# A fused GNN layer on one core: TensorE's step reordered, with ScalarE's step reordered to match

## What is computed

```python
h = relu(layernorm(x))
for t in range(4):                            # edge type
    m = relu(concat(h[src], h[dst]) @ W1[t] + b1[t]) @ W2[t] + b2[t]
    msgs += where(edge_type == t, m, 0)
agg = segment_sum(msgs, dst, num_segments=100000)
i_r, i_z, i_n = split(agg @ W_ih.T + b_ih, 3)
h_r, h_z, h_n = split(h @ W_hh.T + b_hh, 3)
r, z = sigmoid(i_r + h_r), sigmoid(i_z + h_z)
n = tanh(i_n + r * h_n)
out = x + (1 - z) * n + z * h
```

## Time and profile before

| | before |
|---|---|
| median of 3 runs | 1842.27 us (1839.33 to 1843.18) |
| profiled execution: its own time | 1840.2 us |
| its span | 1838.3 us |
| granted TensorE clock, mean | 0.995 |
| PE / DVE / ACT / POOL busy | 91% / 87% / 81% / 64% of the span |
| PE's share of the chain that ended last | 73% |
| data moved | 319.72 MB, 174 GB/s on average |

### The profile page before, as it was taken

One profiled execution on the slowest core, in us unless ns is written; L12 is line 12 of the kernel. 1 busy time (PEld: TensorE's weight loads), 2 busy tenths in 40 slices (PEclk: granted clock), 3 DMA queues, 4 the chain that ended last, 5 costly groups with the idle time before them and its releaser, 6 DMA issues.

```text
span 1838.3 us, 43100 instructions
## 1 busy us (share of the span) xinstructions
PE 1667.1 (91%) x10182; PEld 1416.6 (77%) x10182; DVE 1595.2 (87%) x4186; ACT 1494.6 (81%) x3401; POOL 1178.9 (64%) x1982
## 2 busy tenths in 40 slices
PE   0226799999999999999999999999999999999998
PEld 0125688888888888888888888888888888888787
DVE  8597798989888988898889888989899989898776
ACT  0025789889888898898888888889898889888795
POOL 5777777776776777777765656666666566666310
PEclk9999899999999999999999999999999999999999
DMA  2225677777777776777677777777777777777653
GB/s 70 51 48 139 168 195 194 192 192 192 198 187 193 191 194 186 187 192 191 187 193 187 190 188 187 187 190 189 189 190 188 190 186 192 189 187 191 161 136 100
DMA packets 477071, 319.72 MB, mean 174 GB/s; under 512 B 106705, under 2 KB 463009, under 8 KB 476962
## 3 DMA queue, kind: packets, MB, share of 16 engines
q10 hardware_dynamic: 261792, 156.12, 28.6%
q1 hardware_dynamic: 185730, 106.99, 25.3%
q0 software_dynamic: 29440, 55.47, 11.8%
HBM read 211.65 MB, written 106.72 MB: 173 GB/s over the span
## 4 chain that ended last, share of the span: by engine, by line
PE 73%; ACT 8%; issue 4%; ACTq 3%; DVE 2%; DMA 0%; SPq 0%; POOL 0%; DVEq 0%; POOLq 0%
PE bank L1329 16%; PE bank L1331 12%; PE bank L1330 12%; PE bank L1409 10%; PE bank L1399 5%; PE bank L1391 5%; PE bank L1421 3%; PE bank L1420 3%; PE bank L1437 3%; ACT n_h L1194 3%; PE bank L1447 3%; ACT n_zc L1282 2%; ACTq L1211 2%; ACT e_r L1270 2%; ACTq L1232 2%
## 5 line engine op out<-in xcount | busy, mean ns | idle before, releaser
L580 POOL DMA_INDIRECT e_x<-in_x,rows_now x816 | 799.6, 980 | 241.7 <-issue 233.4
L1177 ACT ACTIVATE e_h<-e_x,shift,rstd 128x128 f32<-128x128 f32 x816 | 355.3, 493 | 93.6 <-DVE shift L1048 93.6
L1194 ACT ACTIVATE n_h<-n_x,shift,rstd 128x128 f32<-128x128 f32 x784 | 362.8, 489 | 2.1 <-issue 2.1
L1329 PE MATMUL bank<-n_h_hi,whh_hi 128*128 128x512 f32 x588 | 263.0, 447 | 25.3 <-ACT n_zc L1282 18.3
L1113 DVE TENSOR_TENSOR n_d<-bank,n_n 128x512 f32<-128x512 f32 x196 | 135.5, 691 | 160.7 <-ACT n_n L1278 149.1
L1329 PE MATMUL bank<-n_a_hi,wih_hi 128*128 128x512 f32 x588 | 249.3, 424 | 0.9 <-DVE bank L1083 0.9
L1071 DVE TENSOR_SCALAR n_sel<-iota,n_rel 128x256 fp32r<-128x256 f32 x784 | 237.8, 365 | 8.6 <-POOL n_rel L631 7.2
L1409 PE MATMUL bank<-n_sel,n_win 128*128 128x256 f32 x1568 | 234.9, 292 | 8.6 <-DVE n_sel L1071 8.4
L1331 PE MATMUL bank<-n_h_hi,whh_lo 128*128 128x512 f32 x588 | 232.9, 396 | 0.0
L1330 PE MATMUL bank<-n_h_lo,whh_hi 128*128 128x512 f32 x588 | 232.7, 396 | 0.0
L1331 PE MATMUL bank<-n_a_hi,wih_lo 128*128 128x512 f32 x588 | 232.3, 395 | 0.0
(11 more groups left out here) (179 smaller groups left out, 3895.4 us busy)
## 6 DMA issues: line engine op xcount, KB each, us to landing
n_win<-messages SPq DMA_DIRECT2D x1568, 64.2 KB
messages<-e_msg ACTq DMA_DIRECT2D x204, 257.0 KB, 2.7
n_x<-in_x ACTq DMA_DIRECT2D x195, 256.0 KB
out<-n_out ACTq DMA_DIRECT2D x195, 256.0 KB
e_x<-in_x,rows_now POOLq DMA_INDIRECT x816
rows_now<-lists SPq DMA_DIRECT2D x204, 2.0 KB
lists<-picks,list_rows POOLq DMA_INDIRECT x72
w<-in_W SPq DMA_DIRECT2D x1, 512.0 KB, 4.5
```

Source lines behind the costliest of these rows:

```text
L580: G.indirect_dma_start(e_x[:, s, 2 * end + t, :], None, x, bass.IndirectOffsetOnAxis(ap=rows_now[:, s, t, end:end + 1], axis=0)).then_inc( ...
L1177: last = A.activation(e_h[:, s % 2, k, :], e_x[:, s, k, :], ACT.Relu, scale=rstd[:, slot, col + k:col + k + 1], bias=shift[:, slot, col + ...
L1194: last = A.activation(n_h[:, s % 2, cols], n_x[:, s, cols], ACT.Relu, scale=rstd[:, slot, col + 4 + k:col + 5 + k], bias=shift[:, slot, co ...
L1329: T.matmul(o, w_hi, v_hi, start=start, stop=False, skip_group_check=onto)
```

## The change

TensorE's step becomes: r gate, hn; node transposes, window sums; z gate, n's second half; hid; back; edge transposes; message. The edge transposes move behind back, z moves ahead of n's second half, both move ahead of hid, and back moves ahead of the message.

ScalarE's step becomes: message copy e_msg (of the unit before: it moves from the end of a step to the start of the next); e_h tiles 0 to 2; n_r; e_h tile 3; store_messages; n_h_hi (it waits for n's second half of the group before instead of for z, as that now comes last of the two); n_h tile 0; n_a_hi; store_out, load_x; n_h tiles 1 and 2; n_zc; n_h tile 3; n_n (tanh); e_r; e_ht. No instruction is added or taken away, and each keeps its semaphores.

```diff
--- before.py
+++ after.py
@@ -1233,6 +1233,12 @@
                                   n_out[:, s, :].rearrange("p (k d) -> p k d", k=TILES)).then_inc(n_stored[s], 16)
 
             def step(i, m):
+                q, s = i - 10, (m - 10) % UNROLL
+                if within(q, UNITS):
+                    act.wait_ge(e_messaged, q + 1)
+                    act.wait_ge(e_tagged, q + 1)
+                    A.activation(e_msg[:, s, :, 0:D], bank[BE1][:, message_part].rearrange("p (t d) -> p t d", t=2),
+                                 ACT.Copy).then_inc(e_high, 1)
                 normalise_edges(i, m, (0, 1, 2))
                 g, s = i - LAG, (m - LAG) % 2
                 if within(g, NG):
@@ -1242,23 +1248,32 @@
                     A.activation(n_r[:, s, :], bank[BRZ][:], ACT.Sigmoid, bias=bsum[:, 0:1]).then_inc(n_red, 1)
                 normalise_edges(i, m, (3,))
                 store_messages(i, m)
-                q, s = i - 8, (m - 8) % 2
-                if within(q, UNITS):
-                    act.wait_ge(e_turned, q + 1)
-                    if due(q - 1):
-                        act.wait_ge(e_hid, q - 1)
-                    A.activation(e_ht[:, s, :], bank[BE0][:], ACT.Copy).then_inc(e_evaced, 1)
                 g, s = i - LAG + 1, (m - LAG + 1) % 2
                 if within(g, NG):
                     act.wait_ge(n_turned, g + 1)
                     if due(g - 1):
-                        act.wait_ge(n_gate_z, g - 1)
+                        act.wait_ge(n_gate_in, g - 1)
                     A.activation(n_h_hi[:, s, :], bank[BT[s]][:], ACT.Copy).then_inc(n_hhi, 1)
+                normalise_nodes(i, m, (0,))
+                if within(g, NG):
                     act.wait_ge(n_summed, g + 1)
                     A.activation(n_a_hi[:, s, :], bank[BA][:], ACT.Copy).then_inc(n_ahi, 1)
-                normalise_nodes(i, m, (0,))
                 store_out(i, m)
                 load_x(i, m)
+                normalise_nodes(i, m, (1, 2))
+                g, s = i - LAG, (m - LAG) % 2
+                if within(g, NG):
+                    act.wait_ge(n_gate_z, g + 1)
+                    if due(g - 1):
+                        act.wait_ge(n_eed, g - 1)
+                    A.activation(n_zc[:, s, :], bank[BRZ][:], ACT.Sigmoid, bias=bneg[:, 1:2],
+                                 scale=-1.0).then_inc(n_zed, 1)
+                normalise_nodes(i, m, (3,))
+                if within(g, NG):
+                    act.wait_ge(n_gate_in, g + 1)
+                    if due(g - 1):
+                        act.wait_ge(n_ded, g - 1)
+                    A.activation(n_n[:, s, :], bank[BIN][:], ACT.Tanh, bias=bih[:, 2:3]).then_inc(n_ned, 1)
                 q, s = i - 9, (m - 9) % 2
                 if within(q, UNITS):
                     act.wait_ge(e_hid, q + 1)
@@ -1269,25 +1284,12 @@
                         kind = 2 * ((m - 9) % 2) + t
                         last = A.activation(e_r[:, s, cols], bank[BE1][:, cols], ACT.Relu, bias=b1_cols[:, kind:kind + 1])
                     last.then_inc(e_relued, 1)
-                normalise_nodes(i, m, (1, 2))
-                g, s = i - LAG, (m - LAG) % 2
-                if within(g, NG):
-                    act.wait_ge(n_gate_in, g + 1)
-                    if due(g - 1):
-                        act.wait_ge(n_ded, g - 1)
-                    A.activation(n_n[:, s, :], bank[BIN][:], ACT.Tanh, bias=bih[:, 2:3]).then_inc(n_ned, 1)
-                    act.wait_ge(n_gate_z, g + 1)
-                    if due(g - 1):
-                        act.wait_ge(n_eed, g - 1)
-                    A.activation(n_zc[:, s, :], bank[BRZ][:], ACT.Sigmoid, bias=bneg[:, 1:2],
-                                 scale=-1.0).then_inc(n_zed, 1)
-                normalise_nodes(i, m, (3,))
-                q, s = i - 9, (m - 9) % UNROLL
+                q, s = i - 8, (m - 8) % 2
                 if within(q, UNITS):
-                    act.wait_ge(e_messaged, q + 1)
-                    act.wait_ge(e_tagged, q + 1)
-                    A.activation(e_msg[:, s, :, 0:D], bank[BE1][:, message_part].rearrange("p (t d) -> p t d", t=2),
-                                 ACT.Copy).then_inc(e_high, 1)
+                    act.wait_ge(e_turned, q + 1)
+                    if due(q - 1):
+                        act.wait_ge(e_hid, q - 1)
+                    A.activation(e_ht[:, s, :], bank[BE0][:], ACT.Copy).then_inc(e_evaced, 1)
 
             pipeline(nc, act, LAST, LOOP_END, step)
 
@@ -1382,14 +1384,6 @@
                     elif due(g):
                         pe.wait_ge(n_ted, g)
                     gate(BHN, 2, s, "h").then_inc(n_gate_hn, 1)
-                q, s = i - 8, (m - 8) % 2
-                if within(q, UNITS):
-                    pe.wait_ge(e_normed, q + 1)
-                    if due(q):
-                        pe.wait_ge(e_evaced, q)
-                    for k in range(4):
-                        last = T.transpose(bank[BE0][:, k * P:(k + 1) * P], e_h[:, s, k, :], ident[:])
-                    last.then_inc(e_turned, 1)
                 g, s = i - LAG + 1, (m - LAG + 1) % 2
                 if within(g, NG):
                     pe.wait_ge(n_normed, g + 1)
@@ -1409,6 +1403,12 @@
                             last = T.matmul(o, n_win[:, w, k, part_ * D:(part_ + 1) * D], n_sel[:, s, k, :],
                                             start=n == 0, stop=n == 3)
                     last.then_inc(n_summed, 1)
+                g, s = i - LAG, (m - LAG) % 2
+                if within(g, NG):
+                    pe.wait_ge(n_red, g + 1)
+                    gate(BRZ, 1, s, "ha").then_inc(n_gate_z, 1)
+                    pe.wait_ge(n_ted, g + 1)
+                    gate(BIN, 2, s, "a", onto=True).then_inc(n_gate_in, 1)
                 q, s = i - 9, (m - 9) % 2
                 if within(q, UNITS):
                     pe.wait_ge(e_evaced, q + 1)
@@ -1420,12 +1420,24 @@
                         T.matmul(o, w1[:, kind, 0, :], e_ht[:, s, t * P:(t + 1) * P], start=True, stop=False)
                         last = T.matmul(o, w1[:, kind, 1, :], e_ht[:, s, (2 + t) * P:(3 + t) * P], start=False, stop=True)
                     last.then_inc(e_hid, 1)
-                g, s = i - LAG, (m - LAG) % 2
-                if within(g, NG):
-                    pe.wait_ge(n_ted, g + 1)
-                    gate(BIN, 2, s, "a", onto=True).then_inc(n_gate_in, 1)
-                    pe.wait_ge(n_red, g + 1)
-                    gate(BRZ, 1, s, "ha").then_inc(n_gate_z, 1)
+                g, s = i - LAG - 1, (m - LAG - 1) % 2
+                if within(g, NG):
+                    pe.wait_ge(n_eed, g + 1)
+                    if within(g + 1, NG):
+                        pe.wait_ge(n_ted, g + 2)
+                    elif due(g):
+                        pe.wait_ge(n_outed, g)
+                    for k in range(TILES):
+                        last = T.transpose(bank[BHN][:, k * P:(k + 1) * P], n_e[:, s, k * P:(k + 1) * P], ident[:])
+                    last.then_inc(n_back, 1)
+                q, s = i - 8, (m - 8) % 2
+                if within(q, UNITS):
+                    pe.wait_ge(e_normed, q + 1)
+                    if due(q):
+                        pe.wait_ge(e_evaced, q)
+                    for k in range(4):
+                        last = T.transpose(bank[BE0][:, k * P:(k + 1) * P], e_h[:, s, k, :], ident[:])
+                    last.then_inc(e_turned, 1)
                 q, s = i - 9, (m - 9) % 2
                 if within(q, UNITS):
                     pe.wait_ge(e_relued, q + 1)
@@ -1436,16 +1448,6 @@
                         o = bank[BE1][:, 2 * P + t * D:2 * P + (t + 1) * D]
                         last = T.matmul(o, e_r[:, s, t * P:(t + 1) * P], w2[:, first + t, :], start=False, stop=t == 1)
                     last.then_inc(e_messaged, 1)
-                g, s = i - LAG - 1, (m - LAG - 1) % 2
-                if within(g, NG):
-                    pe.wait_ge(n_eed, g + 1)
-                    if within(g + 1, NG):
-                        pe.wait_ge(n_ted, g + 2)
-                    elif due(g):
-                        pe.wait_ge(n_outed, g)
-                    for k in range(TILES):
-                        last = T.transpose(bank[BHN][:, k * P:(k + 1) * P], n_e[:, s, k * P:(k + 1) * P], ident[:])
-                    last.then_inc(n_back, 1)
                 if isinstance(i, int) and i == CHECK_STEP:
                     pe.wait_ge(s_odd, 1)
                     T.matmul(bank[BT[0]][0:1, 0:1], ones128[:, 0:1], odd_sum[:], start=True, stop=True
```

## The result

The kernel after takes 1885.41 us (median of 4 runs, 1883.38 to 1887.53) beside 1842.19 us of the kernel before: a ratio of 1.0237, 95% interval 1.022 to 1.0255. It is slower by 43 us; the forecast was 70 us slower. The profiled spans say the same, 1881.5 us against 1838.3 us.

What follows compares the result with a forecast made beforehand. A closed ring of 8.35 us a step bounds the kernel; the new ring sums to 8.66, adding 49 us in the loop, 18 in the head and 3 after it: +70, forecast 1912 us, range 1868 to 1950.

Steps and rivals of the forecast that it cites:

- the sum: New ring in a loop step, from message products through sums, n_a_hi and e_r: 8.66 us against 8.35, averaging 8.72.
- Both rings: Old ring through n_zc (8.35 us) and new ring through the message (8.66), each holding the transfers' issue time.
- The time from n_a_hi to the next activation: On ScalarE, over both issues: 1.31 less 0.10 makes 1.21 us in the loop step, 1.06 in the head.
- The reaction of TensorE to e_r: From e_r's end on ScalarE to the message on TensorE: 0.15 us in the new ring.
- Part (a): z gate and n_zc early: cuts the ring through n_zc, worth at most 0.25 us a step if nothing replaces it.
- Part (e): TensorE's hn weight load: its 132 waits for n_out in the loop, 36.4 us, go away.
- Part (d): Message copy first on ScalarE, with VectorE's e_low: costed at nothing, ready at 4.36 against 4.39 by TensorE's way.
- Rival 1: Second ring through VectorE's n_sel, margin 0.12 us: another 20 to 35 us, 1932 to 1947; chance 0.14.
- Rival 2: Issues hidden, n_a_hi to n_h 0.49, ring 7.94 us, under TensorE's own 8.10: 1800 us; chance 0.08.
- Rival 3: n_h tile 1 comes 0.83 to 0.92 us after n_a_hi, ring 8.28 to 8.37: 1835 to 1880 us; chance 0.13.
- rival 4: Orders written for both engines do not bind, since each semaphore comes early anyway: 1842 us; chance 0.03.
- The signs named for a right forecast: Loop steps 8.65 to 8.75; TensorE waiting 0.3 to 0.5 for e_r; ScalarE idle 0.6 by issue; n_zc, n_out waits gone.

Runs made afterwards that it cites:

- run 2: Kernel after, with load_x alone moved from behind store_out to behind n_zc: 1814.38 us, ratio to before 0.9848.
- run 8: Kernel after, with TensorE's four edge transposes back ahead of the node transposes: 1954.72 us, ratio 1.0632.
- run 6: Kernel after, with n_h tile 0 back behind n_a_hi, ahead of the two issues: 1896.09 us, ratio 1.0299.
- run 3: Kernel after, with store_out and load_x moved from behind n_a_hi to the end of ScalarE's step, behind e_ht: 1865.69 us, ratio to before 1.0127.
- run 7: Kernel after, with ScalarE's e_r moved ahead of the tanh n_n: 1977.27 us, ratio 1.0732.
- run 1: Kernel before, with load_x alone moved from behind store_out to behind the tanh n_n: 1780.59 us, ratio to the kernel before 0.9662.
- half-changed kernels: Kernel before with only TensorE's hunks of the diff (the first), then with only ScalarE's hunks: 2866.35 and 2511.05 us.

## Why the prediction was right, and where it was off

**The direction and the place** were right: slower, by a ring through the message, with both issues uncovered behind n_a_hi. Parts of it were taken away or lengthened one at a time: one issue away gives 71 us back (run 2), 0.43 us more of TensorE's stretch costs 0.38 us (run 8), one more instruction ahead of the issues costs 0.07 us (run 6).

**Term by term**, in the step shown, measured against the sum: message to r gate 0.58 (0.63); r 1.49 (1.47); hn 0.70 (0.70); transposes to sums 0.43 (0.36); sums and reaction 1.26 (1.23); n_a_hi to n_h 1.26 (1.21); the two n_h 0.79 (0.77); n_zc to n_h 0.57, n_h 0.38, tanh to e_r 0.57, both e_r 0.61 (0.57, 0.38, 0.57, 0.62); e_r's end to the message 0.05 (0.15). This step has 8.69 us for the 8.66 of the sum; that the two are so close is in part luck, as the sums 0.07 us late for n_sel make up for a reaction put 0.10 too long.

**The size** was 27 us too large: 13 in the loop (8.63 us a step for the 8.72 of the sum), 10 in the head (8.46 for 8.70), 3 in the steps behind the loop, for which I added 3 and 0.2 came. Two terms were mis-sized.
- The time from n_a_hi to the next activation. "Both rings hold the issue time, so the steps where it is longer keep their excess": that makes 1.27 us on average in the loop and 1.25 in the head, and 1.23 and 1.08 were measured, which is 6 + 7 = 13 us. In the loop the issues are as long as before (load_x 0.42 us on average for 0.43). What is shorter is what stands around them: store_out's issue comes 0.16 us behind n_a_hi's start for 0.28, and n_h 0.05 behind load_x's issue where e_r came 0.10 behind it, together 0.17 where I took off 0.10; the wait for n_xh takes 0.04 of that back. In the head the issue itself took less: the rows below, load_x before and after (ns, least/median/most), have a median of 0.387 for 0.520 us. The idle time behind n_a_hi is 21.3 us over the head's 44 steps, 0.48 us each, where my sum had 0.65 (1.25 less the 0.60 of n_a_hi itself).

```profile
L1211 ACTq DMA_DIRECT2D n_x<-in_x x44: 386/520/1650, 201.7 to 559.1; - x44
```

```profile
L1211 ACTq DMA_DIRECT2D n_x<-in_x x44: 386/387/1272, 201.7 to 566.1; - x44
```

  The same issue thus took between 0.39 and 1.65 us, and the new order changed how often it was long. What makes it long no run took apart.
- The reaction of TensorE to e_r: 0.15 us, taken from n_zc's end to the r gate, where 0.05 was measured, in the head and in the loop: 0.1 us x 180 steps = 18 us. The bias product's start needs less after e_r than the r gate's after n_zc. The other way went the sums, 0.03 us (loop) and 0.04 us (head) later behind the transposes than in the row of before, 6 us.

13 + 18 - 6 = 25 us, with the 3 behind the loop 28 for the 27 found; the other terms are within 0.05 us of what I put.

**Part (a)**, n_zc early: right, its wait is gone; it brought nothing here, as the other ring is longer. **Part (e)**, hn's wait: right, 1 wait for 132. **Part (d)**, the message copy at no cost: nothing in the kernel after speaks against it, but it is close to the edge, as run 3 shows, where the copy came 0.5 us late.

**The rivals.** Rival 1 (VectorE's ring) gave 20 to 35 us more; it is there, but small: the waits list n_sel 5 times, 1.2 us in all, and the 37 steps with late sums make it some 4 us. Runs 3 and 7 show it ready to bind. Rival 2 (the queue gets ahead) fell; where one issue is taken out of the way by hand, the step that it named, TensorE's own, comes about (run 1, and many steps of run 2). Rival 3 fell with the 1.23 us on average from n_a_hi to n_h (it needed 0.83 to 0.92), rival 4 with the 134 waits for e_r. The signs named for a right forecast are all there but two: the loop's step is 8.63 us, just under the 8.65 to 8.75 given, and the idle time behind n_a_hi is put down to "issue" only for 40.9 of its 86.1 us.

What stays open: why the new order with one issue moved is still 34 us behind the old order with the same edit. The waits point to n_rel on GpSimd; no run changed that alone.

## What to carry to other kernels

When several engines are nearly full, look for the closed ring of waits and sum it from starts, and do it again for the new order before you believe that a removed wait is a gain; the reordering here traded a ring of 8.36 us for one of 8.63. Look at what stands ahead of a transfer issued from a compute engine's queue. Where that was an instruction waiting for a semaphore, as here, only the instruction's own 0.60 us covered the issues, and the rest of their time fell on the engine; put it behind one that does not wait and has work ahead of it (moving one such line was worth 61 us in the kernel before and 71 us in the kernel after). Do not read such idle time as time that other work could fill for free: giving the engine work to do there (run 6) made the kernel slower, as the queue had one more instruction to pass.

## What the runs showed that I had not expected

- A row of idle time names what came last, not what cost the time: 45.2 of the 86.1 us behind n_a_hi are put down to VectorE's n_xh and shift, of which n_xh delayed an issue by up to 0.09 us in all steps but one (0.38), 0.04 on average, and the two issues made the rest.
- I had not listed load_x's wait for n_xh at all: the new order brings the issue nearer to it.
- The same issue of load_x had medians of 0.520 and 0.387 us in the heads of the two kernels.
- In the half-changed kernels TensorE's clock went back and forth between its two levels, full and half. In the first of them it stood at half from 1007.7 to 1011.1 us, after TensorE had waited 2.55 us before a message product and then, but for its last 0.1 us, a wait of 1.18 us before the r gate; a step later it did so again. In the kernel after, with 0.38 us of waiting a step, it kept 1.00 from 554 to 1703 us.
